# Head pairs in cross attention, one bank for a head's turned blocks in self attention, and two products for the delta sums

## What is computed

```
x = x + L0_attn(layernorm(x))         # causal self attention, 16 heads in 4 groups of 4, HD = 128, rope
x = x + L0_xattn(layernorm(x), ctx)   # attention to a few set vectors
x = x + L0_ffn(layernorm(x))          # 16 routed experts
x = x + L1_attn(layernorm(x))         # delta rule with decay and gates, 16 key heads
x = x + L1_xattn(layernorm(x), ctx)   # cross attention: keys are 64 context vectors and the 256 tokens
x = x + L1_ffn(layernorm(x))          # 128 routed experts, 48 kept
```

## Time and profile before

| what | value |
|---|---|
| median of the runs | 4089.55 us |
| the profiled execution's own time | 4080.05 us |
| its span, first to last instruction | 4078.2 us |
| mean granted clock of TensorE | 0.932 of full speed |
| TensorE matmul busy | 3568.7 us, 88% of the span |
| VectorE, ScalarE, GpSimd busy | 2668.5, 1676.4, 1407.4 us |
| self attention, about 30 to 650 us | TensorE busy 572.77 of 620 us |
| cross attention, about 2903 to 3815 us | TensorE busy 838.04 of 912 us |

### The profile page before, as it was taken

One profiled execution on the slowest core, in us unless ns is written; L12 is line 12 of the kernel. 1 busy time (PEld: TensorE's weight loads), 2 busy tenths in 40 slices (PEclk: granted clock), 3 DMA queues, 4 the chain that ended last, 5 costly groups with the idle time before them and its releaser, 6 DMA issues. The chain is left out here.

```text
span 4078.2 us, 59075 instructions
## 1 busy us (share of the span) xinstructions
PE 3568.7 (88%) x17488; PEld 2739.0 (67%) x17488; DVE 2668.5 (65%) x7918; ACT 1676.4 (41%) x4266; POOL 1407.4 (35%) x2115
## 2 busy tenths in 40 slices
PE   7999997499688999999999999998499999999665
PEld 5767675355366888888888888886366666666453
DVE  5666665622257888888888888873676676676521
ACT  3444443233234554555545455541244444444221
POOL 0000000078515555555555555553111111111055
PEclk9999998599778999999999999999699999999765
DMA  2000004245501111111111111110100000000456
GB/s 77 0 0 0 0 0 112 77 80 83 108 14 28 36 35 30 37 27 37 27 38 27 39 28 37 28 21 11 59 1 0 0 0 0 0 0 0 118 119 138
DMA packets 220952, 150.06 MB, mean 37 GB/s; under 512 B 116976, under 2 KB 208656, under 8 KB 220208
## 3 DMA queue, kind: packets, MB, share of 16 engines
q1 hardware_dynamic: 193664, 111.55, 10.8%
q0 software_dynamic: 22848, 31.69, 4.7%
q10 hardware_dynamic: 4224, 4.19, 0.3%
HBM read 105.71 MB, written 41.61 MB: 36 GB/s over the span
## 5 line engine op out<-in xcount | busy, mean ns | idle before, releaser
L1998 DVE SCALAR_TENSOR_TENSOR dl_y<-ps,dl_taps,dl_y 128x255 f32<-128x255 f32 (+2 forms) x1536 | 653.2, 475 | 128.5 <-ACT dl_y L1894 124.3
L1729 PE MATMUL ps<-xnT,dl_wkqv 128*128 128x256 f32 x2048 | 543.3, 391 | 29.8 <-DVE dl_lp L2041 21.6
L1729 PEld LDWEIGHTS ps<-xnT,dl_wkqv 128*128 128x128 f32 x2048 | 368.8, 194 | 81.2 <-issue 35.4
L519 PE MATMUL ps<-at_shared,at_v 128*128 128x256 f32 (+2 forms) x1280 | 320.9, 382 | 56.4 <-DVE at_shared L689 29.4
L1652 POOL TENSOR_TENSOR dl_rn<-dl_n,mhalf 128x4 f32<-128x4 f32 x128 | 173.1, 1352 | 550.4 <-DVE dl_n L2014 550.4
L519 PEld LDWEIGHTS ps<-at_shared,at_v 128*128 128x128 f32 (+1 forms) x1280 | 206.5, 188 | 164.6 <-issue 111.2
L431 POOL TENSOR_TENSOR at_rs<-at_ss,mhalf 64x1 f32<-64x1 f32 x32 | 55.4, 1731 | 742.3 <-DVE at_ss L623 742.3
L1894 ACT ACTIVATE dl_y<-ps,dl_taps 128x256 f32<-128x256 f32 x512 | 260.1, 559 | 103.1 <-PE ps L1729 103.1
L454 PE MATMUL ps<-at_wq,at_xb 128*128 (+1 forms) x512 | 244.8, 612 | 39.6 <-POOL at_xb L425 33.8
L1670 POOL TENSOR_TENSOR dl_inv_u<-dl_inv_u,dl_inv_tmp 64x30 f32<-64x30 f32 (+14 forms) x480 | 260.7, 543 | 37.6
L490 PE MATMUL ps<-at_kT,at_qT 128*128 128x320 f32 (+2 forms) x1024 | 257.7, 385 | 1.4 <-ACT at_kT L745 1.4
(11 more groups left out here) (362 smaller groups left out, 7935.6 us busy)
## 6 DMA issues: line engine op xcount, KB each, us to landing
dl_grow<-decay_rows SPq DMA_DIRECT2D x128, 128.0 KB, 3.1
sp_wgu<-in_w1gu SPq DMA_DIRECT2D x12, 768.0 KB, 5.8
dl_wkqv<-in_w1kqv SPq DMA_DIRECT2D x16, 512.0 KB, 4.6
delta_diag<-dl_lp SPq DMA_DIRECT2D x512, 8.0 KB
dl_diag<-delta_diag_tt SPq DMA_DIRECT2D x512, 8.0 KB, 1.7
moe_wgu<-in_w0gu SPq DMA_DIRECT2D x16, 448.0 KB, 12.0
sp_wd<-in_w1d SPq DMA_DIRECT2D x12, 384.0 KB, 6.8
dl_wo<-in_w1o SPq DMA_DIRECT2D x16, 256.0 KB, 3.7
```

What stands on the lines that cost most here:

```text
L519: last = nc.tensor.matmul(slot(h, (r % 2) * 4 + 3)[:, c0:S], v[h][0:w, j, :], pT[h][0:w, r % 2, j, c0:S], start=j == 0, stop=j == KT - 1)
L1729: last = nc.tensor.matmul(bank(h, m // 2, (m % 2) * S, (m % 2 + 1) * S), wkqv[h][:, c, m * P:(m + 1) * P], k.xnT[:, c, u.seq * S:(u.seq + ...
L1998: last = nc.vector.scalar_tensor_tensor(y[h][:, m, back:S], bank(h, m // 2, (m % 2) * S, (m % 2 + 1) * S - back), taps[h][:, m, KC - 1 - b ...
```

## The change

**Self attention.** Transposed blocks are written so that all three of a head lie in one bank, as 384 columns, and ScalarE copies them in one instruction. VectorE copies nothing there any more, and `mix` waits for ScalarE alone.

**Cross attention.** The context is laid out twice, on 128 partitions: it is projected with 128 rows, rotated, squared, normed and turned with 128. Probabilities of an even head are stored as tokens then context and those of the odd head beside it as context then tokens (the keys are kept as context, tokens, context so that either order is a plain slice). The context columns of a pair are then neighbours, 128 wide, and one transpose for each query tile turns both. They are turned after the token blocks of the odd head, and VectorE copies them once for the pair (`keep_context`). `mix` of an even head does its two token products before it waits for that copy; `mix` of the odd head uses partitions 64 to 127 of it. GpSimd copies the context twice into `xb`, and ScalarE copies 64 key columns more.

**Delta.** The 24 small products for the sums become one with the triangular matrix over all 256 columns and one with ones over 128 columns, and the wait for `made` stands after them.

```diff
                 def turn_probs(h, u, r):
...
+                    if cross:
                         for t in range(TB):
+                            pe.wait_ge(s.probs_ready[h], u * (G * TB) + (r * TB + t + 1))
+                            for j in range(TB):
+                                last = nc.tensor.transpose(slot(h, (r % 2) * 4 + j)[:, t * P:(t + 1) * P],
+                                                           own(h, r, t)[:, j * P:(j + 1) * P], k.ident[:, :])
+                        last.then_inc(s.probs_turned[h], 1)
+                        if r % 2:
+                            for t in range(TB):
+                                last = nc.tensor.transpose(slot(h, 6)[:, t * P:(t + 1) * P], context_pair(h, t), k.ident[:, :])
+                            last.then_inc(s.pair_turned[h], 1)
+                    else:
+                        pe.wait_ge(s.probs_ready[h], u * G + (r + 1))
+                        for t in range(TB):
+                            for j in range(t + 1):
+                                last = nc.tensor.transpose(slot(h, (r % 2) * 4 + j)[:, (t - j) * P:(t - j + 1) * P],
+                                                           prob(h, r, t)[:, j * P:(j + 1) * P], k.ident[:, :])
+                        last.then_inc(s.probs_turned[h], 1)
 
                 def mix(h, u, r):
+                    o = slot(h, (r % 2) * 4 + 3)
                     pe.wait_ge(s.probs_kept_a[h], u * G + (r + 1))
-                    pe.wait_ge(s.probs_kept_d[h], u * G + (r + 1))
-                    for j in range(KT):
-                        w = krows[j]
+                    if cross and r % 2:
+                        pe.wait_ge(s.probs_kept_d[h], u * 2 + (r // 2 + 1))
+                    for j in range(TB):
                         c0 = 0 if cross else j * P
-                        last = nc.tensor.matmul(slot(h, (r % 2) * 4 + 3)[:, c0:S], v[h][0:w, j, :],
-                                                pT[h][0:w, r % 2, j, c0:S], start=j == 0, stop=j == KT - 1)
+                        last = nc.tensor.matmul(o[:, c0:S], v[h][:, j, :], pT[h][:, r % 2, j, 0:S - c0],
+                                                start=j == 0, stop=not cross and j == TB - 1)
+                    if cross:
+                        if r % 2 == 0:
+                            pe.wait_ge(s.probs_kept_d[h], u * 2 + (r // 2 + 1))
+                        n0 = (r % 2) * CTX
+                        last = nc.tensor.matmul(o, v[h][n0:n0 + CTX, TB, :], pT[h][n0:n0 + CTX, 0, TB, :], start=False, stop=True)
                     last.then_inc(s.mixed[h], 1)
...
-                def keep_probs(h, u, r):
-
-                    dve.wait_ge(s.probs_turned[h], u * G + (r + 1))
-                    piece = slot(h, (r % 2) * 4 + 2)
-                    if cross:
-                        last = nc.vector.tensor_copy(pT[h][0:CTX, r % 2, TB, :], piece[0:CTX, :])
-                    else:
-                        last = nc.vector.tensor_copy(pT[h][:, r % 2, 1, P:S], piece[:, P:S])
-                    last.then_inc(s.probs_kept_d[h], 1)
+                def keep_context(h, u, r):
+                    dve.wait_ge(s.pair_turned[h], u * 2 + (r // 2 + 1))
+                    nc.vector.tensor_copy(pT[h][:, 0, TB, :], slot(h, 6)).then_inc(s.probs_kept_d[h], 1)
...
-                    nc.gpsimd.tensor_tensor(rs[h][0:CTX, TB, G:G + 1], ss[h][0:CTX, TB, G:G + 1], k.mhalf[0:CTX, 0:1], ALU.pow)
+                    nc.gpsimd.tensor_tensor(rs[h][:, TB, G:G + 1], ss[h][:, TB, G:G + 1], k.mhalf[:, 0:1], ALU.pow)
...
-                    nc.scalar.copy(kT[h][:, :], k.ps[h][:, 2, 0:NK]).then_inc(s.qk_kept[h], 1)
+                    if cross:
+                        nc.scalar.copy(kT[h][:, 0:CTX], k.ps[h][:, 2, S:NK])
+                        nc.scalar.copy(kT[h][:, CTX:CTX + NK], k.ps[h][:, 2, 0:NK]).then_inc(s.qk_kept[h], 1)
+                    else:
+                        nc.scalar.copy(kT[h][:, :], k.ps[h][:, 2, 0:NK]).then_inc(s.qk_kept[h], 1)
...
-                        last = nc.scalar.copy(pT[h][:, r % 2, 0, :], slot(h, (r % 2) * 4))
+                        last = nc.scalar.copy(pT[h][:, r % 2, :, :].rearrange("p j s -> p (j s)")[:, 0:S + P],
+                                              k.ps[h][:, (r % 2) * 2, 0:S + P])
...
                 pe.wait_ge(loaded, 16 * 5)
-                pe.wait_ge(made, 1)
...
                 pe.wait_ge(loga_ready, 1)
-                for i in range(NT):
-                    o = k.ps[0][:, 1, i * HK:(i + 1) * HK]
-                    last = nc.tensor.matmul(o, tri[:, :], loga[:, i, :], start=True, stop=i % TB == 0)
-                    if i % TB:
-                        last = nc.tensor.matmul(o, ones[:, :], loga[:, i - 1, :], start=False, stop=True)
-                last.then_inc(cum_ready, 1)
+                sums = k.ps[0][:, 1, 0:NT * HK]
+                by_tile = sums.rearrange("p (b t e) -> p b t e", t=TB, e=HK)
+                nc.tensor.matmul(sums, tri[:, :], loga[:, :, :].rearrange("p t e -> p (t e)"), start=True, stop=False)
+                nc.tensor.matmul(by_tile[:, :, 1, :], ones[:, :], loga[:, :, :].rearrange("p (b t) e -> p b t e", t=TB)[:, :, 0, :],
+                                 start=False, stop=True).then_inc(cum_ready, 1)
+                pe.wait_ge(made, 1)
                 pe.wait_ge(cum_kept, 1)
```

More of the change, by code:

```diff
@@ L288, in __init__ @@
         self.probs_turned = k.sems("probs_turned")
+        self.pair_turned = k.sems("pair_turned")
         self.probs_kept_a = k.sems("probs_kept_a")
@@ L334, in sb @@
             return k.sb(f"at{k.attn_calls}_{name}", shape, dt, st)
-        xb = [sb(f"xb{h}", [P, DC, NK]) for h in range(2)]
+        xb = [sb(f"xb{h}", [P, DC, KT * P]) for h in range(2)]
         t1 = [sb(f"t1{h}", [P, KT, G + 1, HD]) for h in range(2)]
@@ L339, in attention @@
         qT = [sb(f"qT{h}", [P, G, S]) for h in range(2)]
-        kT = [sb(f"kT{h}", [P, NK]) for h in range(2)]
+        kT = [sb(f"kT{h}", [P, CTX + NK if cross else NK]) for h in range(2)]
         v = [sb(f"v{h}", [P, KT, HD]) for h in range(2)]
@@ L367, in ckv_ps, with prob, own, context_pair @@
         def ckv_ps(h, part):
-            return k.ps[h][0:CTX, 3, part * HD:(part + 1) * HD]
+            return k.ps[h][:, 3, part * HD:(part + 1) * HD]
         def slot(h, m):
             return k.ps[h][:, m // 2, (m % 2) * S:(m % 2) * S + S]
-        pieces = (0, 1, 2) if cross else (0, 2)
         def seen(t):
             return NK if cross else (t + 1) * P
+        def prob(h, r, t):
+            return probs[h][:, t * 2 + r % 2, 0:NK] if cross else probs[h][:, (r % 2) * TB + t, 0:seen(t)]
+        def own(h, r, t):
+            return prob(h, r, t)[:, (r % 2) * CTX:(r % 2) * CTX + S]
+        def context_pair(h, t):
+            return probs[h][:, :, :].rearrange("p m s -> p (m s)")[:, t * 2 * NK + S:t * 2 * NK + S + 2 * CTX]
+        def keys(h, r, t):
+            c0 = CTX * (1 - r % 2) if cross else 0
+            return kT[h][:, c0:c0 + seen(t)]
         def scores(h, r, t):
@@ L424, in take_tokens @@
                     if cross:
-                        xc = nc.gpsimd.tensor_copy(xb[h][:, :, S:NK], ctx.ctxT[:, :, ds(turn(u) * (2 * CTX) + h * CTX, CTX)])
+                        for c0 in (S, S + CTX):
+                            xc = nc.gpsimd.tensor_copy(xb[h][:, :, c0:c0 + CTX],
+                                                       ctx.ctxT[:, :, ds(turn(u) * (2 * CTX) + h * CTX, CTX)])
                     xc.then_inc(s.xb_ready[h], 1)
@@ L490, in score @@
                         last = nc.tensor.matmul(scores(h, r, t), qT[h][:, r, t * P:(t + 1) * P],
-                                                kT[h][:, 0:seen(t)], start=cross, stop=cross or t == TB - 1)
+                                                keys(h, r, t), start=cross, stop=cross or t == TB - 1)
                         if cross:
@@ L497, in turn_probs @@
                 def turn_probs(h, u, r):
-                    for t in range(TB):
-                        if cross:
-                            pe.wait_ge(s.probs_ready[h], u * (G * TB) + (r * TB + t + 1))
-                        elif t == 0:
-                            pe.wait_ge(s.probs_ready[h], u * G + (r + 1))
-                        for j in range(TB):
-                            if cross or j <= t:
-                                last = nc.tensor.transpose(slot(h, (r % 2) * 4 + pieces[j])[:, t * P:(t + 1) * P],
-                                                           probs[h][:, (r % 2) * TB + t, j * P:(j + 1) * P], k.ident[:, :])
@@ L603, in rotate @@
                         cc, sc = rope.c(turn(u), h)
-                        last = each(t1[h][0:CTX, TB, G, :], t2[h][0:CTX, TB, G, :], ckv_ps(h, 0), cc, sc)
+                        last = each(t1[h][:, TB, G, :], t2[h][:, TB, G, :], ckv_ps(h, 0), cc, sc)
                     last.then_inc(s.rotated[h], 1)
@@ L611, in add_halves @@
                     if cross:
[L612 to L613 removed]
```

(13 more changed lines are left out.)

38 lines of the change are left out of this document (15 added, 23 removed).

## The result

The changed kernel takes 4137.81 us (median of 3 runs, 4128.42 to 4146.96) against 4089.55 us: a ratio of 1.0119, 95% interval [1.0082, 1.0156]. It is 1.2% slower, where 0.8% faster was forecast. The profiled execution took 4146.96 us, its span is 4145.2 us, and the mean granted clock fell from 0.932 to 0.910.

What follows compares the result with a forecast made beforehand. It took TensorE's work and its waits inside a stage to bound the kernel. Savings of 11 us in self attention, 12 in cross attention and 11 in delta gave 4055.5 us, range 4042 to 4072.

Steps and rivals of the forecast that it cites:

- (6): Cross attention, second half: saved turns, copies and waits are worth nothing, becoming a longer wait before head 3's `mix`.
- rival B: Cross attention, second half: waits merge into one of 1.2 to 1.6 us, TensorE's clock falls; 4135 at 0.91; chance 0.04.
- (1): Self attention, first half: ScalarE's copy grows from 256 to 384 columns and `mix` waits for it, +0.12 us.
- (3): Self attention, second half: VectorE's copies leave and TensorE is free earlier, saving 0.27 us a stage.
- (2): Self attention, first half: VectorE's copies leave, head 2's maxima come 0.20 us earlier; net of ScalarE's longer copy, 0.08.
- (4): Cross attention, first half: two narrow transposes no longer precede ScalarE's copy, so `mix` starts 0.22 us earlier.
- (5): Cross attention: the context's key turn uses 128 rows, not 64, so the q projection starts earlier, saving 0.16 us.
- step 8: Cross attention, norm chain: GpSimd's power on 128 x 1 was taken as 1731 ns, no change.
- rival C: Cross attention: power on 128 partitions scales with partitions, 1.73 us more on the norm chain, 4109 us; chance 0.02.
- step 9: Cross attention: `mix` on partitions 64 to 127 was taken as unchanged from partitions 0 to 63.
- (10): Delta's start: TensorE started only after GpSimd's `made`, while ScalarE could start earlier; 2.1 us saved.
- (11): Delta sums: 48 instructions become four, so VectorE's wait shrinks from 10.52 to 1.6 us, 8.9 us less.

Runs made afterwards that it cites:

- old_gap: Kernel before the change, with three unread ScalarE copies delaying head 3's blocks in cross attention: 4136.51 us, ratio 1.0114 to the kernel before.
- fill1_give: Changed kernel with one unread product behind head 3's `mix`, in the wait before `give`: 4092.33 us, ratio 1.0015 to the kernel before.
- fill1_mix: Changed kernel with one unread product in the gap ahead of head 3's `mix`: 4067.07 us, ratio 0.9954 to the kernel before.
- split_wait: Changed kernel, but an even head's `mix` waits for the pair's context copy before all its products: 4083.38 us, ratio 1.0006 to the kernel before.
- cross_old: Changed kernel with the old cross attention, so only the self attention and delta parts are new: 4066.37 us, ratio 0.9946 to the kernel before.
- fill3: Changed kernel with three unread products between the `mix` of head 2 and of head 3: 4056.26 us, ratio 0.9924 to the kernel before.
- copy_first: Changed kernel, but in cross attention ScalarE copies head 3's blocks ahead of `keep_v`: 4056.64 us, ratio 0.9925 to the kernel before.
- late_tokens: Changed kernel, but in self attention GpSimd's token copy waits until q and k are turned: 4123.58 us, ratio 1.0091 to the kernel before.

## Why the prediction was wrong

What TensorE's idle time in cross attention did, in one table (us, from one trace of each; "falls" counts, of 28 stages, those in which `give` took over 4 us, against 3.72; 0.56/0.61 are the two sets of buffers in turn; 0 is under 0.1):

| run | before head 2's mix | before head 3's | before `give` | before `turn_qk` | falls | stage |
|---|---|---|---|---|---|---|
| changed kernel | 0 | 1.40 | 0.56/0.61 | 0 | 28 | 30.02 |
| old_gap | 0.95 | 0.88 | 0.56/0.61 | 0 | 10 | 29.47 |
| fill1_give | 0 | 1.40 | 0 | 0 | 13 | 28.60 |
| fill1_mix | 0 | 0.77 | 0.56/0.61 | 0 | 3 | 27.72 |
| split_wait | 0.86 | 0.34 | 0.56/0.61 | 0 | 1 | 28.16 |
| cross_old | 0.95 | 0.23 | 0.56/0.61 | 0 | 0 | 27.89 |
| fill3 | 0 | 0 | 0.56/0.61 | 0 | 0 | 27.56 |
| copy_first | 0 | 0 | 0.56/0.61 | 1.54 | 0 | 27.56 |

**The step that failed** is the end of (6): "What is saved there turns into a longer wait in front of head 3", priced at nothing, and with it the weight of 0.04 for rival B. B named the mechanism, the place (one wait of 1.2 to 1.6; it is 1.40) and nearly the time: 4135 at a clock of 0.91; measured were 4137.81 and 0.90. (By B's formula 0.90 costs 0.10 x 890 = 89 us, somewhat more than the 76 below; part of the lower clock falls on idle time, as in the window at 3326.60 above.) The prediction's own sign of being wrong, a granted clock below 0.98, came true with it. B was set aside because "the stage already holds waits of nearly 1 us at 0.99". That sentence compared the length of one wait, and the rows showed none above 0.95, so nothing read from the trace covered a wait of 1.2 to 1.6, and the prediction's words that "gaps of this size leave the clock up" claimed more than the rows held. fill1_give and old_gap show that the neighbours of the wait count too: 0.95 followed by 0.23 and 0.56 is harmless, 0.95 followed by 0.88 and 0.56 is not, and 1.54 before `turn_qk` is harmless. No single measure puts the table in order: not the longest wait (0.95 has 10 falls or none), and not the sum of the three before `give` (about 1.8 has none in cross_old, 1.40 has 13 in fill1_give). What is shown is that the clock is lost by idle time in the second half of a stage, ahead of `give`, and comes back when that is filled or moved; the exact condition stays open. The price follows from rows: 30.02 - 27.56 = 2.46 us a stage, times 31 is 76 us, and the ratios of the changed kernel and of copy_first are 0.0194 or 79 us apart. Most of it is `give`, 5.95 in the mean of 28 stages instead of 3.72; the rest is head 3's `mix`. The Trainium skill's page "TensorE: Matmul & The Clock Gate", Part 1, tells of a kernel in which short idle times between groups of matmuls make the clock swing between its two levels; the trace agrees, with idle times of 1.40 and 0.61 us and a clock of 1.00 and 0.53 within one stage.

**Steps (1) to (3), self attention: right in mechanism, too large.** ScalarE's copy is 0.48 (forecast 0.49), and `mix` in the first half waits 0.24 for it. `turn_qk` waits for nothing, as it already did in the trace before. But the stage gained 0.17, not 0.35. The first half gave 0.10, nearly the 0.08 of steps (1) and (2); the second gave 0.07 instead of the 0.27 of (3). The term that was off is the start of head 3's turns: I let head 3's chain run at the durations of before, while its division, 0.67 then, now starts earlier in GpSimd's token copy and takes 0.84. Those 0.17 are nearly all of what is missing. late_tokens takes the whole hold-up away, the 0.12 of before as well, and the gain becomes 0.44. A rule fits this: the Trainium skill's page "SBUF — State Buffer", section "Who interferes with whom", says that VectorE's `tensor_scalar` can contend with GpSimd for a shared pair of ports; the trace agrees that VectorE's division is held up beside the copy, by 0.12 us before and 0.29 now, while GpSimd's copy keeps its length. One reading was taken from the wrong half, but no term hangs on it: VectorE's two copies take 0.62 in the first half, and the 0.47 are those of the second.

**Steps (4), (5), cross attention: right.** From the first half's turns to `mix` it is 3315.58 - 3314.31 = 1.27 now and 3308.80 - 3307.31 = 1.49 in cross_old, so 0.22 as forecast. From `turn_qk` to the scores it is 3.10 against 3317.22 - 3313.96 = 3.26 in the earlier trace rows, so 0.16 as forecast. The stage gained 0.33 of these 0.38 where the clock held. The unmeasured costs were well bounded: the power on 128 x 1 takes 1725 ns (step 8 took 1731), which ends rival C, and the context product on partitions 64 to 127 takes 0.70 like the one on 0 to 63 (step 9).

**Steps (10), (11), delta: right.** 2.15 us at the start and 8.8 at the sums: VectorE starts 1.69 us after the first of the two products (forecast 1.36 + 0.2 = 1.56).

So the sum of the forecast, 34 us, held apart from the clock: copy_first stands 31 us (24 to 38) below the kernel before. Part of that is luck. The stages and the start of delta account for 5 + 10 + 11 = 26 us; self attention gave less than forecast, and delta, run alone, gave more (14 to 25 us) for reasons that are in part open.

## What to carry to other kernels

Where the granted clock is full but TensorE idles in several pieces close together, as here, take the clock as something that may be at its edge: price a change that shifts or merges these pieces at the lower clock for the work behind them, not at nothing, and compare the whole neighbourhood of the gap with what the trace has shown harmless, not the longest wait. If the clock falls, look for an order on another engine that moves the idle time elsewhere (here ScalarE had 1.09 us free ahead of `keep_v`) before adding work to fill it. And when an engine's work is moved earlier by a few tenths, look at what GpSimd does in the new place.

## What was not expected of the hardware

- Adding six matmuls a stage that nothing reads made the kernel 1.9% faster (fill3), and adding 0.7 us of ScalarE copies to the kernel before cost 1.1%, over 40 us, of which the delay itself explains about 13 (28.3 - 27.9 = 0.4 a stage).
- An identical pattern of waits lets the clock fall in some stages and not in others, and not at random. In fill1_give five stages with the fall and five without follow each other. In old_gap the falls repeat after ten stages. In the changed kernel `give` takes about 5.2, 5.6, 6.0, 6.3 and 6.7 us in turn, over and over. What sets this rhythm, and why 1.54 to 1.79 us before `turn_qk` never did harm, the runs do not settle.
- GpSimd's power takes 1725 ns for one value a partition, 1096 for four, 1958 for ten and 3917 for fifteen: merging two calls into one saved nothing.
